# A graph attention kernel: each 128-edge unit's source rows gathered once into a ring in SBUF, and copied from there for every pair

## The reference

```python
h_l = (features @ weight_l).reshape(num_nodes, HEADS, OUT_F)   # 4 heads of 32
h_r = (features @ weight_r).reshape(num_nodes, HEADS, OUT_F)
x_i = h_l[tgt]
x_j = h_r[src]
e = jnp.sum(jax.nn.leaky_relu(x_i + x_j, NEG_SLOPE) * att, axis=-1)
seg_max = jax.ops.segment_max(e, tgt, num_segments=num_nodes)
exp_e = jnp.exp(e - seg_max[tgt])
seg_sum = jax.ops.segment_sum(exp_e, tgt, num_segments=num_nodes)
alpha = exp_e / jnp.clip(seg_sum[tgt], 1e-16)
out = jax.ops.segment_sum(x_j * alpha[..., None], tgt, num_segments=num_nodes)
```

## Time and profile before

| | us |
|---|---|
| median of 3 runs | 3264.74 (3261.08 to 3267.59) |
| span of the profiled execution | 3261.1 |
| PE busy, share of span | 3095.5, 95% |
| POOL busy, share of span | 927.4, 28% |
| attention stage, first gather to first load of the next stage | 687.2 to 1246.3 |

### The profile page before, as it was taken

The page is one execution under the profiler, slowest core; times in us unless marked ns, Lnnn a source line. Parts: engine busy times, 40 slices in busy tenths (PEclk is TensorE's granted clock), DMA queues, the critical chain, the costliest instruction groups (busy, mean ns, idle before and its releaser), DMA issues. The chain is left out here.

```text
span 3261.1 us, 45319 instructions
## 1 busy us (share of the span) xinstructions
PE 3095.5 (95%) x14598; PEld 2015.9 (62%) x14598; DVE 1336.6 (41%) x3053; ACT 1396.7 (43%) x2506; POOL 927.4 (28%) x1063
## 2 busy tenths in 40 slices
PE   7979999979999997999999999999999999999998
PEld 6865555557888885777777555555555555555554
DVE  7960111126666667999999411111111111111112
ACT  6950001235555555888887423333332222223333
POOL 4530000047777763777777100000000000000000
PEclk9989999988998898999999999999999999999999
DMA  2666667623333323666666566666666677777774
GB/s 82 262 241 265 266 276 290 268 59 81 89 85 82 83 66 96 192 193 188 185 184 178 229 283 283 283 283 283 283 283 283 283 292 290 293 290 294 291 299 164
DMA packets 165548, 709.30 MB, mean 218 GB/s; under 512 B 38135, under 2 KB 131938, under 8 KB 152271
## 3 DMA queue, kind: packets, MB, share of 16 engines
q1 hardware_dynamic: 126713, 618.83, 49.2%
q0 software_dynamic: 33600, 83.09, 9.3%
q10 hardware_dynamic: 5011, 4.48, 0.5%
HBM read 657.91 MB, written 48.07 MB: 216 GB/s over the span
## 5 line engine op out<-in xcount | busy, mean ns | idle before, releaser
L1448 PE MATMUL deep_out_psum<-deep_adjacency,deep_scaled_nodes_odd 125*128 125x450 f32 (+1 forms) x1750 | 669.7, 537 | 0.0
L1448 PE MATMUL deep_out_psum<-deep_adjacency,deep_scaled_nodes 125*128 125x450 f32 (+1 forms) x1750 | 669.7, 537 | 0.0
L1696 POOL DMA_INDIRECT source_rows<-gat_source_rows,pair_src x416 | 395.8, 952 | 574.9 <-POOLq L64 448.5
L1448 PEld LDWEIGHTS deep_out_psum<-deep_adjacency,deep_scaled_nodes_odd 125*128 125x128 f32 x1750 | 328.4, 189 | 299.8 <-issue 298.9
L1448 PEld LDWEIGHTS deep_out_psum<-deep_adjacency,deep_scaled_nodes 125*128 125x128 f32 x1750 | 328.1, 189 | 298.9 <-issue 298.0
L2126 POOL DMA_INDIRECT near_room<-gate_source_rows,pair_src x416 | 395.5, 951 | 141.7 <-issue 124.1
L1506 ACT ACTIVATE deep_squares_high<-deep_aggregate,deep_vectors 128x450 fp32r<-128x450 f32 (+1 forms) x70 | 46.8, 668 | 618.0 <-DVE deep_aggregate L1578 618.0
L1448 PE MATMUL gcn_out_psum<-adjacency_columns,gcn_scaled_nodes 125*128 125x450 f32 (+1 forms) x700 | 268.9, 538 | 0.0
L2229 PE MATMUL gate_banks<-edge_weights,edge_features_t 128*128 128x256 f32 x832 | 248.4, 380 | 0.0
L1448 PEld LDWEIGHTS gcn_out_psum<-adjacency_columns,gcn_scaled_nodes 125*128 125x128 f32 x700 | 131.3, 190 | 123.6 <-issue 123.0
L1592 DVE SCALAR_TENSOR_TENSOR deep_normed<-deep_aggregate,deep_vectors,deep_squares 128x450 f32<-128x450 f32 (+1 forms) x70 | 47.9, 685 | 384.9 <-ACT deep_squares L1515 384.9
(11 more groups left out here) (423 smaller groups left out, 4927.6 us busy)
## 6 DMA issues: line engine op xcount, KB each, us to landing
deep_adjacency<-adjacency SPq DMA_DIRECT2D x69, 5625.0 KB, 16.2
adjacency_columns<-adjacency SPq DMA_DIRECT2D x19, 5625.0 KB, 16.2
adjacency<-adjacency_columns SPq DMA_DIRECT2D x7, 5625.0 KB, 17.7
edge_features<-in_edge_attr_dram SPq DMA_DIRECT2D x416, 64.0 KB
att_node_rows<-pair_dst_rows SPq DMA_DIRECT2D x104, 128.0 KB, 3.2
gate_node_rows<-pair_dst_rows SPq DMA_DIRECT2D x104, 128.0 KB, 3.4
source_rows<-gat_source_rows,pair_src POOLq DMA_INDIRECT x416
near_room<-gate_source_rows,pair_src POOLq DMA_INDIRECT x416
```

What stands on the lines that cost most here:

```text
L1448: m = nc.tensor.matmul(op[:, n % 2, 0:cols], h[l % 2][:, s, :], ring[0:T, n % 2, s, 0:cols], start=s == 0, stop=s == NS - 1)
L1696: pool.indirect_dma_start(xj[:, b % HOLD, q, :], None, d["h_r"], bass.IndirectOffsetOnAxis(ap=c["pair_src"][:, b * PQ + q:b * PQ + q + 1], ...
```

## The change

POOL gathers each of the 391 units once (392 gathers with a blank one) into `held`, a ring of 48 units. Before each gather it waits for the landing of the one six before it, so the count of gathers issued, `s_gi`, tells how many have landed: unit u has when the count is u + 7. Every fourth gather waits as well for the copies that free its place. SP loads for each block four ring places and one count into registers (`pair_words`, rows 32 and 64), waits for the count and for the place in `xj` (HOLD is now 11 blocks), and issues four copies of 128 x 512 B from `held` to `xj`. PE waits for the copies. The row loads `dr` are issued two blocks further ahead. `pair_src` goes to DRAM and comes back, with the next stage's weights, for the gate stage. The tables take ten more small operations on VectorE behind block 4, one more behind block 10, and four transposes on PE behind block 9.

```diff
+UNITS_HELD = 48
+UNITS_GATHERED = NU + 1
+LANDED_BEHIND = 6
...
         if n == 9:
+            act.wait_ge(self.s_dl, 2)
+            act.dma_start(self.d["pair_src"], self.pair_src[:, :]).then_inc(self.s_st, 16)
...
             pe.wait_ge(self.s_bm, 2)
+            for t in range(UTL):
+                nc.tensor.transpose(ps[:, 0, t * 128:(t + 1) * 128], self.src_f[:, t, :], c["ident"][:, :])
...
+            vec.tensor_scalar(c["pair_words"][64:65, :], self.unit[64:65, :], 1.0 + LANDED_BEHIND, None, ALU.add)
+            self.o.link(vec.tensor_scalar(self.turns[:, :], self.unit[32:33, :], float(UNITS_HELD), None, ALU.is_ge))
+            for k in range(2, (UNITS_GATHERED - 1) // UNITS_HELD + 1):
+                self.o.link(vec.scalar_tensor_tensor(self.turns[:, :], self.unit[32:33, :], float(k * UNITS_HELD), self.turns[:, :], ALU.is_ge, ALU.add))
+            self.o.link(vec.scalar_tensor_tensor(c["pair_words"][32:33, :], self.turns[:, :], -float(UNITS_HELD), self.unit[32:33, :], ALU.mult, ALU.add))
...
             dve.wait_ge(self.s_bt, 1)
+            vec.tensor_copy(c["unit_src"][:, 0:UNITS_GATHERED], ps[:, 0, 0:UNITS_GATHERED])
...
-HOLD = BEHIND + 6
+HOLD = BEHIND + 3
...
+        held = sb("unit_rows", [128, UNITS_HELD, D])
...
-            for b in range(NPB):
-                if b >= HOLD:
-                    pool.wait_ge(s_msg, b - HOLD + 1)
-                for q in range(PQ):
-                    pool.indirect_dma_start(xj[:, b % HOLD, q, :], None, d["h_r"],
-                                            bass.IndirectOffsetOnAxis(ap=c["pair_src"][:, b * PQ + q:b * PQ + q + 1], axis=0)).then_inc(s_g[b % HOLD], 16)
-            for b in range(NPB - HOLD, NPB):
-                pool.wait_ge(s_g[b % HOLD], 16 * PQ * (b // HOLD + 1))
+            def landed(u):
+                pool.wait_ge(s_g[u % len(s_g)], 16 * (u // len(s_g) + 1))
+            for u in range(UNITS_GATHERED):
+                if u >= LANDED_BEHIND:
+                    landed(u - LANDED_BEHIND)
+                done = (u + PQ - UNITS_HELD + NS - 1) // PQ - 1
+                if u % PQ == 0 and done >= 0:
+                    pool.wait_ge(s_cp[done % HOLD], 16 * PQ * (done // HOLD + 1))
+                pool.indirect_dma_start(held[:, u % UNITS_HELD, :], None, d["h_r"], bass.IndirectOffsetOnAxis(ap=c["unit_src"][:, u:u + 1], axis=0),
+                                        engine_sem=s_gi).then_inc(s_g[u % len(s_g)], 16)
+            pool.wait_ge(s_gi, UNITS_GATHERED)
+            for u in range(UNITS_GATHERED, UNITS_GATHERED + LANDED_BEHIND):
+                landed(u - LANDED_BEHIND)
+                pool.sem_inc(s_gi, 1)
...
+            def copies(b):
+                slot = four(nc, sp, c["pair_words"][32:33, :], b, UNITS_HELD - 1)
+                last = sp.value_load(c["pair_words"][64:65, b * PQ + PQ - 1:b * PQ + PQ], min_val=1, max_val=UNITS_GATHERED + LANDED_BEHIND)
+                if b >= HOLD:
+                    sp.wait_ge(s_msg, b - HOLD + 1)
+                sp.wait_ge(s_gi, last)
+                for q in range(PQ):
+                    sp.dma_start(xj[:, b % HOLD, q, :], held[:, bass.ds(slot[q], 1), :].rearrange("e o f -> e (o f)")).then_inc(s_cp[b % HOLD], 16)
...
+                if b == 0:
+                    node_rows(0)
+                    node_rows(1)
+                if b + 2 < NPB:
+                    node_rows(b + 2)
+                copies(b)
...
-                pe.wait_ge(s_g[b % HOLD], 16 * PQ * (b // HOLD + 1))
+                pe.wait_ge(s_cp[b % HOLD], 16 * PQ * (b // HOLD + 1))
...
+        eng.dma_start(self.pair_src[:, :], pair_src).then_inc(self.s_w, 16)
...
-                                            bass.IndirectOffsetOnAxis(ap=c["pair_src"][:, b * PQ + q:b * PQ + q + 1], axis=0)).then_inc(s_g[b % 4], 16)
+                                            bass.IndirectOffsetOnAxis(ap=br.pair_src[:, b * PQ + q:b * PQ + q + 1], axis=0)).then_inc(s_g[b % 4], 16)
```

More of the change, by code:

```diff
@@ L730, in __init__ @@
         self.passed = room[0:NS - 1, NS * D + 2 * KP:NS * D + 3 * KP]
+        self.turns = room[32:33, NS * D + 2 * KP:NS * D + 3 * KP]
+        self.pair_src = self.unit.bitcast(I32)
         self.work = sb("path_work", [128, 16 * 128])
@@ L863, in vector @@
             vec.tensor_scalar(self.shift[:, :], ps[:, 1, 0:KP], float(T), None, ALU.mult)
-            vec.tensor_copy(c["pair_tile"][:, :], ps[0:1, 1, 0:KP])
+            vec.tensor_copy(c["pair_words"][0:1, :], ps[0:1, 1, 0:KP])
             vec.tensor_scalar(c["pair_node"][:, :], ps[0:1, 1, 0:KP], float(T), None, ALU.mult)
-            self.o.link(vec.tensor_scalar(c["pair_edge"][:, :], self.unit[0:1, :], 128.0, None, ALU.mult))
+            vec.tensor_scalar(c["pair_edge"][:, :], self.unit[0:1, :], 128.0, None, ALU.mult)
+            vec.tensor_scalar(c["pair_words"][64:65, :], self.unit[64:65, :], 1.0 + LANDED_BEHIND, None, ALU.add)
[3 more added lines that the diff above has]
+            self.o.link(vec.scalar_tensor_tensor(c["pair_words"][32:33, :], self.turns[:, :], -float(UNITS_HELD), self.unit[32:33, :], ALU.mult, ALU.add))
         if n == 6:
@@ L1675, in attention @@
          s_fl, s_dp, s_c, s_cc, s_hf, s_tp, s_d, s_k, s_kk, s_sl, s_x, s_w, s_wc, s_msg, s_A, s_rs, s_O, s_hv) = (c["sems"].take("att_" + n) for n in names)
-        s_g = [c["sems"].take(f"att_sources_gathered_{k}") for k in range(HOLD)]
+        s_gi = c["sems"].take("att_gathers_issued")
+        s_g = [c["sems"].take(f"att_unit_gathered_{k}") for k in range(LANDED_BEHIND + 2)]
+        s_cp = [c["sems"].take(f"att_sources_copied_{k}") for k in range(HOLD)]
         s_dr = [c["sems"].take(f"att_node_rows_loaded_{k}") for k in range(4)]
@@ L1706, in _, with node_rows @@
         def _(sp):
+            def node_rows(b):
+                if b >= 4:
+                    sp.wait_ge(s_oht, b - 3)
+                sp.dma_start(dr[:, b % 4, :], d["pair_dst"][b * PQ:(b + 1) * PQ, :].rearrange("k e -> (k e)").unsqueeze(0).to_broadcast([128, L])
+                             ).then_inc(s_dr[b % 4], 16)
+            def copies(b):
[6 more added lines that the diff above has]
+                    sp.dma_start(xj[:, b % HOLD, q, :], held[:, bass.ds(slot[q], 1), :].rearrange("e o f -> e (o f)")).then_inc(s_cp[b % HOLD], 16)
             with nc.allow_non_contiguous_dma(reason="one value to a partition"):
@@ L1730, in terms @@
             def terms(b):
-                tile = four(nc, pe, c["pair_tile"], b, NS - 1)
+                tile = four(nc, pe, c["pair_words"][0:1, :], b, NS - 1)
                 pe.wait_ge(s_oht, b + 1)
-                pe.wait_ge(s_g[b % HOLD], 16 * PQ * (b // HOLD + 1))
+                pe.wait_ge(s_cp[b % HOLD], 16 * PQ * (b // HOLD + 1))
                 if b >= 2:
@@ L1981, in merge @@
             def merge(b):
-                tile = four(nc, dve, c["pair_tile"], b, NS - 1)
+                tile = four(nc, dve, c["pair_words"][0:1, :], b, NS - 1)
                 s = b // PER_SB
@@ L2026, in __init__, with load @@
         self.att_bias = sb("attention_bias", [128, 1])
+        self.pair_src = sb("gate_pair_src", [128, KP], I32)
         self.s_w, self.s_n = (c["sems"].take("bridge_" + n) for n in ("weights_loaded", "weights_negated"))
-    def load(self, eng, nc, w_f, w_s, b_f, b_s, att_bias):
+    def load(self, eng, nc, w_f, w_s, b_f, b_s, att_bias, pair_src):
         for t in range(2):
@@ L2540, in graph_network @@
         attention(nc, c, d, a["L1_gnn_att"], rows, acc,
-                  lambda sp: br.load(sp, nc, wf, ws, a["L2_gnn_b_f"], a["L2_gnn_b_s"], a["L1_gnn_bias"]))
+                  lambda sp: br.load(sp, nc, wf, ws, a["L2_gnn_b_f"], a["L2_gnn_b_s"], a["L1_gnn_bias"], d["pair_src"]))
         target = sb("gate_target_rows", [T, PARTS, NS, 2 * D], BF16)
```

18 lines of the change are left out of this document (8 added, 10 removed).

## The result

The changed kernel takes 3300.74 us (3299.21 to 3302.51, 4 runs) where the one before takes 3262.91 us (3260.25 to 3267.59, 4 runs): ratio 1.0114, 95% interval 1.0102 to 1.0126, slower by 38 us. The forecast was 3267 with a range up to 3284. The profiled execution has a span of 3297.5 us, 36.4 more than before.

What follows compares the result with a forecast made beforehand. PE was taken to pace the attention stage behind block 14, at 4.62 us a block plus low clock, gathers only early. Terms 7.2 - 5.2 + 0.5 = +2.5 us on 3264.7 gave 3267, range 3251 to 3284.

Steps and rivals of the forecast that it cites:

- the costing of SyncE's queue: Attention stage: SP's row load, register loads, four copies and break rows take 3.7 us a block, under PE's 4.62.
- rival C: Attention loop: SP or the copies pace it, at worst 6.7 us a block, +175 us; chance 0.03.
- The threshold: Attention loop: SP or the copies decide the pace above 4.62 us a block, PE's pace at full clock.
- Start: Attention stage: block 0 on PE waits for ten gathers and its copies, so starts at 705.0, +8.7 us.
- the transposes: First layers: four more transposes on PE, which bounds there, cost +0.5 us.
- Blocks 0 to 9: Attention stage: still paced by gathers, two gathers saved at tile borders, -2.5 us; block 9 comes +7.2 us.
- Blocks 9 to 103: Attention stage: PE's own pace with its gather waits gone, -5.2 us, low clock left as it is.
- Gathers: POOL, attention stage: 392 gathers at 1.25 us from 687, last issued about 1179; added waits cost nothing.
- Rival D: Attention stage: added waits cost POOL 0.08 us a gather, so gathers get no faster: 3272; chance 0.05.
- A: Attention stage: PE's low-clock stretches become fewer and gathers bound, block 103 29.5 us sooner: 3236; chance 0.18.
- B: Attention stage: late start and worse clock, 5.19 us a block behind block 9, +16 us: 3281; chance 0.27.
- The sum: Whole kernel: 7.2 - 5.2 + 0.5 = +2.5 us, a median of 3267.

Runs made afterwards that it cites:

- constant slots: Changed kernel with each copy's ring place and count as constants, no register loads on SyncE, most pairs getting rows of other edges: 3261.30 us, ratio 0.9996.
- the dose: Changed kernel with one more register load a block on SyncE, its value unused: 3357.52 us, ratio 1.0302.

## Why the prediction was wrong

**The step that failed** is the costing of SyncE's queue: "3.7 us, under PE's 4.62". It was the right step to take, and rival C named the right mechanism and a threshold ("decides above 4.62 us a block"), with a chance of 0.03. The terms were too small, every one:

| term, us a block | forecast | measured |
|---|---|---|
| row load | 0.33 | 0.55 (0.59 behind copies, 0.42 behind break rows; 0.33 where SyncE had idled) |
| registers, between row load and copies | 0.51 + 0.5 | 1.44 |
| four copies | 1.88 | 2.43 |
| break rows | 0.47 | 0.51 |
| gaps, slow issues, waits | 0 | 0.05 + 0.22 + 0.04 |
| sum | 3.7 | 5.24 |

The rows for all of it came from the gate stage, where SyncE isn't full: 2.72 us of a block's 4.72. The 0.333 us of a copy there is one whose source is DRAM; a copy out of SBUF takes 0.5 to 0.6, even where SyncE has time to spare (constant slots). The 0.47 for the break rows is misread as well: 1.88 us are three pitches and one issue, so the pitch is 0.52. Nearly 1 us of margin looked safe; three terms were 0.2 to 0.55 us short, and slow issues and gaps, put at nothing, took another 0.3. The range made it worse: C was priced only at its worst case (+175 us), not at the case just above the threshold. Its signs came as named: SP at 5.24 us a block and not under 4, and PE waiting for copies all along.

The threshold itself is rough. 4.62 us is PE at full clock; on average PE takes 5.04 (constant slots) to 5.10 us a block, more than SyncE's 4.98 without its slow issues. The slow issues (0.22 us a block) are about as large as what lies between 5.04 and the measured 5.28, but how two paces so close together add up was not tested.

**Start:** +8.7 from the first gather to block 0 was forecast, +8.9 measured. Right; another 4.4 came ahead of the first gather (0.8 to 3.2 in the six other profiled executions at the usual pace), of which the transposes were 0.4 (forecast 0.5); what the rest is wasn't looked into.

**Blocks 0 to 9:** -2.5 was forecast, +4.8 came. The copies of blocks 0 and 9 are issued 46.96 us apart, 5.22 a block, and behind block 0 SyncE waits for less than 2 us, so it paced here too. With constant slots it is 43.6 against 44.15, 0.5 less and not 2.5.

**Blocks 9 to 103:** -5.2 was forecast, +16.9 came, from SyncE as shown. With constant slots -5.0 came in the profiled execution. That is near the 5.2, but the reading behind it isn't borne out: the kernel before waits at its first transposes for 2.4 us in all from 740 to 1220, about half of what the prediction worked out, and with constant slots 1.4 us are left from 767 to 1220 (0.9 before). What made up the rest of the 5.0 us isn't shown.

**Gathers:** the pitch between waits is 1.25 us. The added waits on POOL, put at nothing, cost 15.0 us in all from 767 to 1220, where the copies that free a place were late; the last gather is issued at 1195.5, where 1179 was forecast, and nothing depends on it. With constant slots POOL waits for nothing and the pitch is 1.26. Rival D is out, as forecast.

**Rivals A and B:** the clock in 767 to 1200 is 0.93 against 0.91, and 0.91 when the changed kernel was run again. Neither the return of the full clock (A) nor a worse one (B) happened. B's late start did come, and its sign of a loss, 5.09 us a block or more, too, but by SyncE. With constant slots PE waits for copies 1.4 us in 767 to 1220, and the clock is 0.91. The Trainium skill ("TensorE: Matmul & The Clock Gate", section "HAM oscillation — how this bites in real kernels") tells of a loop in which waits for DMAs bring the low clock in every round. The trace doesn't test that: the kernel before had hardly such waits to lose (0.9 us in 767 to 1220), and its low stretches stayed without them. Added waits went both ways: 16.9 us for copies in 767 to 1220 with a clock of 0.93 (changed kernel), 41.6 us with 0.88 (the dose).

**The sum** would have come out right by its total: with SyncE's stream made short, the kernel is at 0.9996 of before (0.9979 to 1.0013), where the forecast of +2.5 us is 1.0008. Part of that is luck: block 0 came 11.0 us late and not 8.7, blocks 0 to 9 won 0.5 us and not 2.5, and the 5.2 us of waits were only half there.

**Forms that beat both kernels** weren't found. Constant slots is equal to before, and only a plan known ahead could have them. Moving issues to ScalarE gave back 21 of the 38 us with the break rows, and lost nearly all of that again with the row loads.

## What to carry to other kernels

Before work is moved to a queue that only issues DMAs, write out its stream for one round of the loop, with register loads, register operations and asserts, and compare it with the round; "busy" shows none of it, and an issuing engine that never waits in the trace is full. Take prices from rows of the same kind (source memory, and behind a full queue), and where margin is less than a third of the sum, price the case just past the threshold and give it a real chance. To prove who paces, add a dose to the suspected engine alone: 0.55 us a block for 0.59 us of dose settled here what the view of PE's waits called only "issue".

## What the hardware showed that I had not expected

- A DMA issue on SyncE for 128 x 512 B out of SBUF: 0.51 us with the register operation beside it, 0.64 apart; with constant addresses 0.60 and still 0.64 apart. From DRAM rows in the gate stage 0.33, and 0.52 apart.
- The same row load takes 0.33 us where SyncE had idled, 0.42 behind break rows, 0.59 behind copies.
- A register load on SyncE takes 0.28 to 0.50 us in this loop (0.30 for four words in the gate stage), and the bounds check with its register operations 0.3 more.
- 100 row loads put on ScalarE between its activations cost the kernel 20 us, though ScalarE was busy for about half of the stage. Whether by the issues or by the waits ahead of them isn't separated.
